# Turning the adapter probabilities by a crossbar transpose in float16 pieces instead of on TensorE

## What is computed

```
xn  = layernorm(x)
q,k,v: 16 query heads of 16 channels share one key and one value head
att = softmax(q k^T) v, turned back to 256 channels, times Wo, plus bo
# adapter, six experts e with 100 rows l of rank 16: A (6,100,16), B (6,16,256)
tokens = A B                             # (e, l, c)
p      = softmax(xn tokens^T / 16)       # over the 100 rows, per expert
delta  = ((p[1:] val[1:]) + xn) wd^T + wd_b, times scale   # val = tokens wt^T + wt_b
ffn    = xn + log(exp(delta of the expert that the gate picks)), 0 replaced by eps
out    = x + att + ffn
```

## Time and profile before

| | |
|---|---|
| runs | 920.78, 924.08, 924.17 us |
| profiled execution | 922.81 us |
| its span (first to last instruction) | 921.0 us |
| mean granted TensorE clock | 0.971 of 2.4 GHz |
| busy: PE / DVE / ACT / POOL | 857.4 / 780.7 / 673.2 / 512.8 us |
| period of one batch, windows 1 to 13 | 52.40 us, 0.82 us a slot |

### The profile page before, as it was taken

How to read it: one execution, slowest core, us unless ns; L and a number is a source line. 1 busy time by engine, 2 the same in 40 slices (tenths; PEclk the granted TensorE clock), 3 DMA queues, 4 the chain that set the end, 5 groups by cost and what they waited for, 6 DMA issues and landing times.

```text
span 921.0 us, 17722 instructions
## 1 busy us (share of the span) xinstructions
PE 857.4 (93%) x5845; PEld 282.1 (31%) x5845; DVE 780.7 (85%) x1490; ACT 673.2 (73%) x1369; POOL 512.8 (56%) x691
## 2 busy tenths in 40 slices
PE   4479999999999999999999999999999999999895
PEld 2223222332323333332323333332333333232222
DVE  6578898988989898998989898998989898899814
ACT  2115787787878778777877877787778778788880
POOL 2656566565666656565666647566666656534200
PEclk9676999999999999999999999999999999999998
DMA  3423243534524453543335353442444453331110
GB/s 96 97 66 60 74 92 92 117 83 116 113 75 105 107 114 94 124 87 108 95 94 111 94 116 87 129 100 86 96 113 104 104 115 84 92 94 61 48 60 34
DMA packets 125072, 86.04 MB, mean 93 GB/s; under 512 B 57143, under 2 KB 109112, under 8 KB 124984
## 3 DMA queue, kind: packets, MB, share of 16 engines
q1 hardware_dynamic: 124824, 84.82, 38.3%
q10 hardware_dynamic: 160, 0.10, 0.1%
HBM read 39.30 MB, written 33.54 MB: 79 GB/s over the span
## 4 chain that ended last, share of the span: by engine, by line
PE 78%; DVE 15%; issue 3%; POOL 2%; ACT 1%; DMA 1%; ACTq 0%; POOLq 0%; DVEq 0%
PE pO L364 24%; PE pA L346 18%; DVE M L808 9%; PE pB L351 8%; PE pA L481 5%; PE pA L428 5%; PE pA L499 4%; PE pA L483 3%; PE pA L417 3%; PE pA L453 2%; PE pA L468 2%; DVE st L728 2%; PE pB L461 1%; DVE RL L821 1%; PE pB L439 1%
## 5 line engine op out<-in xcount | busy, mean ns | idle before, releaser
L808 DVE TENSOR_REDUCE M<-pA 128x1 f32<-128x512 f32 x1024 | 652.3, 682 | 86.4 <-PE pA L346 82.3
L627 ACT ACTIVATE P<-pB 128x512 f32<-128x512 f32 x1002 | 552.6, 601 | 130.5 <-PE pB L351 126.0
L346 PE MATMUL pA<-K,Q 48*128 48x512 f16 x1024 | 326.0, 388 | 21.7 <-DVE M L808 11.8
L351 PE MATMUL pB<-Q,K 50*128 50x512 f16 x1002 | 317.8, 385 | 0.3 <-DVE M L808 0.3
L364 PE MATMUL pO<-P,VK 128*32 128x512 f32 x2048 | 273.7, 607 | 3.1 <-ACT OTr L633 2.0
L346 PEld LDWEIGHTS pA<-K,Q 48*128 48x128 f16 x1024 | 67.8, 94 | 343.6 <-DVE M L808 287.7
L954 POOL TENSOR_SCALAR Cz<-Cx 128x512 f32<-128x512 f32 x32 | 62.1, 1940 | 37.0 <-ACT Cx L609 37.0
L499 PE MATMUL pA<-wo,On 128*128 128x256 f32 x248 | 71.9, 414 | 2.7 <-DVE RL L821 2.7
L364 PEld LDWEIGHTS pO<-P,VK 128*32 128x32 f32 x2048 | 40.4, 108 | 99.3 <-issue 63.2
L351 PEld LDWEIGHTS pB<-Q,K 50*128 50x128 f16 x1002 | 64.3, 94 | 11.8 <-ACT P L627 10.3
L968 POOL TENSOR_TENSOR On<-Op,Rb 128x512 f32<-128x512 f32 x31 | 39.9, 1286 | 45.0 <-issue 41.2
(11 more groups left out here) (148 smaller groups left out, 806.6 us busy)
## 6 DMA issues: line engine op xcount, KB each, us to landing
o_parts<-OTr SPq DMA_DIRECT2D x62, 256.0 KB, 2.3
X<-in_x SPq DMA_DIRECT2D x16, 512.0 KB, 3.9
q_pieces<-Qp SPq DMA_DIRECT2D x64, 128.0 KB
out<-OUT SPq DMA_DIRECT2D x32, 256.0 KB, 3.9
Op<-o_parts SPq DMA_DIRECT2D x31, 256.0 KB
Rb<-l_parts SPq DMA_DIRECT2D x31, 256.0 KB
Q<-q_pieces SPq DMA_DIRECT2D x30, 256.0 KB, 4.8
Q<-q_pieces SPq DMA_DIRECT2D x34, 128.0 KB, 4.5
```

What stands on the lines that cost most here:

```text
L346: e.matmul(bank1("ab", t)[:, :], Q16[r:r + 48, b % 3, h, 128 * s:128 * s + 128], K16[r:r + 48, b % 3, :], start=True, stop=True).then_inc( ...
L351: e.matmul(bankB(t)[:, :], K16[r:r + 50, b % 3, 128 * i:128 * i + 128], Q16[r:r + 50, b % 3, :, 32 * hh:32 * hh + 32], start=True, stop=Tr ...
L627: e.activation(P[:, u % PR, :], bankB(u + LB)[:, :], ACT.Exp, scale=alpha).then_inc(S("e"))
L808: e.tensor_reduce(M[:, t // 32 % 2, t % 2, t % 32 // 2:t % 32 // 2 + 1], bank1("ab", t)[:, :], AX, ALU.max, negate=True).then_inc(S("mx"))
```

## The change

En is split in two float16 pieces by two more GpSimd instructions inside `snorm` (a cast and a subtraction) into EP, 128 x 2 x 4 x 128; a new step `pd` on SP, slot 52.2 (12.6 for the first batch), turns EP by one crossbar transpose of 8 blocks to PT; `a` becomes three float16 products of 512 columns with the pieces of A. The steps `p` (TensorE) and `pte` (ScalarE) are gone, and with `p` one turn of the pB ring per batch. A power-of-two scale for the pieces is worked in: VectorE's sums are multiplied by 2^-11 before the reciprocal, VectorE's mask product takes one more factor, the largest element of A joins the search for the scale at the start, and GpSimd splits A once, in the step `ams` at slot -30, behind `utm` of batch 0. The load of Am_s moves from SP to ScalarE's queue.

```diff
-    "smax": -20.4, "sexp": -18.8, "ssum": -17.4, "snorm": -16.2, "p": -13, "pte": -12.4, "a": -5, "mm": -4.4,
+    "smax": -20.4, "sexp": -18.8, "ssum": -17.4, "snorm": -16.2, "pd": -11.8, "a": -5, "mm": -4.4,
...
# TensorE
-                if (b := due("p", n)) is not None:
-                    w.wait_ge(*before2("p", b))
-                    w.wait_ge(S("en"), b + 1)
-                    for i in range(4):
-                        mm = e.transpose(bank2("p", b)[0:NL, 128 * i:128 * i + 128], En[:, i, :], idf[:, :])
-                    mm.then_inc(S("pt"))
                 if (b := due("a", n)) is not None:
                     w.wait_ge(*before1("a", b))
-                    w.wait_ge(S("pte"), b + 1)
-                    w.wait_ge(S("am"), 16)
-                    e.matmul(bank1("a", b)[0:ER + 1, :], Am_s[0:NL, :], PT[0:NL, :],
-                             start=True, stop=True).then_inc(S("ma"))
+                    w.wait_ge(S("ptd"), 16 * (b + 1))
+                    w.wait_ge(S("amp"), 2)
+                    for k, (ap, pp) in enumerate(PIECES):
+                        mm = e.matmul(bank1("a", b)[0:ER + 1, :], AmP[0:NL, ap, :], PT[0:NL, pp, :, :],
+                                      start=(k == 0), stop=(k == 2))
+                    mm.then_inc(S("ma"))
...
# ScalarE
+            w.wait_ge(S("am0"), 1)
+            e.dma_start(Am_s[1:NL, 0:ER], Am[1:NL, :]).then_inc(S("am"), 16)
...
-                if (b := due("pte", n)) is not None:
-                    w.wait_ge(S("pt"), b + 1)
-                    w.wait_ge(S("ma"), b)
-                    e.copy(PT[0:NL, :], bank2("p", b)[0:NL, :]).then_inc(S("pte"))
...
# VectorE
+                    e.memset(amx[:, 1:2], 0.0).then_inc(S("am3"))
+                    w.wait_ge(S("am"), 16)
+                    w.wait_ge(S("am3"), 1)
+                    e.tensor_reduce(amx[0:NL, 1:2], Am_s[0:NL, 0:ER], AX, ALU.max,
+                                    apply_absolute_value=True).then_inc(S("wm"))
...
                     w.wait_ge(S("en"), b)
+                    e.tensor_scalar(sL[:, :], sL[:, :], 2.0 ** -11, None, ALU.mult).then_inc(S("sl2"))
+                    w.wait_ge(S("sl2"), b + 1)
                     e.reciprocal(sR[:, :], sL[:, :]).then_inc(S("sr"))
...
-                    e.tensor_tensor(MmT[0:ER + 1, :], bank1("a", b)[0:ER + 1, :], mkT[0:ER + 1, :],
-                                    ALU.mult).then_inc(S("mm"))
+                    e.scalar_tensor_tensor(out=MmT[0:ER + 1, :], in0=bank1("a", b)[0:ER + 1, :], scalar=asc[0:ER + 1, 0:1],
+                                           in1=mkT[0:ER + 1, :], op0=ALU.mult, op1=ALU.mult).then_inc(S("mm"))
...
# GpSimd
                     w.wait_ge(S("sr"), b + 1)
-                    w.wait_ge(S("pt"), b)
                     e.tensor_tensor(En[:, :, :], Es[:, :, :], bc(sR[:, :], NL), ALU.mult).then_inc(S("en"))
+                    w.wait_ge(S("en"), b + 1)
+                    w.wait_ge(S("ptd"), 16 * b)
+                    w.wait_ge(S("ep0"), 1)
+                    e.tensor_copy(EP[:, 0, :, 0:NL], En[:, :, :]).then_inc(S("eh"))
+                    w.wait_ge(S("eh"), b + 1)
+                    e.tensor_tensor(EP[:, 1, :, 0:NL], En[:, :, :], EP[:, 0, :, 0:NL], ALU.subtract).then_inc(S("el"))
+
+                if due("ams", n) is not None:
+                    w.wait_ge(S("scl"), 1)
+                    w.wait_ge(S("am"), 16)
+                    w.wait_ge(S("amd"), 1)
+                    e.memset(asc[:, :], 2.0 ** -11).then_inc(S("asc"))
+                    w.wait_ge(S("asc"), 1)
+                    e.tensor_copy(asc[0:ER, :], scl[0:ER, 7:8]).then_inc(S("asc"))
+                    e.tensor_scalar(Am_s[0:NL, 0:ER], Am_s[0:NL, 0:ER], scl[0:NL, 3:4], None, ALU.mult).then_inc(S("asc"))
+                    w.wait_ge(S("asc"), 3)
+                    e.tensor_copy(AmP[0:NL, 0, :], Am_s[0:NL, :]).then_inc(S("amp"))
+                    w.wait_ge(S("amp"), 1)
+                    e.tensor_tensor(AmP[0:NL, 1, :], Am_s[0:NL, :], AmP[0:NL, 0, :], ALU.subtract).then_inc(S("amp"))
...
# SyncE
+                if (b := due("pd", n)) is not None:
+                    w.wait_ge(S("el"), b + 1)
+                    w.wait_ge(S("ma"), b)
+                    e.dma_start_transpose(PT[:, :, :, :].rearrange("p k i t -> p (k i) t"),
+                                          EP[:, :, :, :].rearrange("p k i n -> p (k i n)")).then_inc(S("ptd"), 16)
```

More of the change, by code:

```diff
@@ L53 @@
     "qs1": -50, "vg": -50, "vge": -49, "vt": -48, "vte": -47, "gate": -46, "mask": -45, "qw1": -40, "mkd": -39,
-    "utm": -30, "s": 5, "smax": 5.6, "sexp": 6.2, "ssum": 6.8, "snorm": 7.4, "p": 13, "pte": 13.6, "a": 17, "mm": 17.6,
+    "utm": -30, "s": 5, "smax": 5.6, "sexp": 6.2, "ssum": 6.8, "snorm": 7.4, "pd": 12.6, "a": 17, "mm": 17.6,
     "d0": 21, "dexp0": 21.6, "d1": 25, "dexp1": 25.6, "guard0": 26.8, "dlog0": 30.2, "radd0": 31.6,
@@ L70 @@
     "rngq": -92, "rng": -88, "rg": -87, "xt0": -86.9, "xt1": -86.8, "xh0": -86.7, "xh1": -86.6, "two": -86.5, "xl0": -86.2,
-    "bs": -86, "scl": -85.8, "xl1": -85.6, "wh": -85.4, "wl": -85.2, "alpha": -60, "qra": -53.5, "qrb": -38, "wdh": -35, "scd": -35,
+    "bs": -86, "scl": -85.8, "xl1": -85.6, "wh": -85.4, "wl": -85.2, "alpha": -60, "ams": -30, "qra": -53.5, "qrb": -38, "wdh": -35, "scd": -35,
     "bw0": -34, "bwe0": -33.4, "bw1": -33.8, "bwe1": -33.3, "w2": -25, "w2e": -24.4, "w2s": -24.2,
@@ L79 @@
 PARTH_LAST = {"lr": 86.2, "or": 86.3, "rec": 88.8, "lw": 89.4, "rb": 92.2, "on": 98.3}
-PE_NAMES = ("ab", "pv", "rg", "xt0", "xt1", "bs", "bw0", "bw1", "w2", "uk", "q0", "q1", "vg", "vt", "s", "p", "a", "d0", "d1",
+PE_NAMES = ("ab", "pv", "rg", "xt0", "xt1", "bs", "bw0", "bw1", "w2", "uk", "q0", "q1", "vg", "vt", "s", "a", "d0", "d1",
             "d2", "d3", "mt", "o0", "o1", "o2", "o3", "sl0", "sl1", "oa0", "oa1", "oa2", "oa3", "ob0", "ob1", "ob2", "ob3")
-ACT_NAMES = ("root", "xh0", "xh1", "wh", "wdh", "kd", "alpha", "bwe0", "bwe1", "w2e", "qe0", "qe1", "vge", "vte", "sexp", "pte", "dexp0",
+ACT_NAMES = ("root", "xh0", "xh1", "wh", "wdh", "kd", "alpha", "bwe0", "bwe1", "w2e", "qe0", "qe1", "vge", "vte", "sexp", "dexp0",
              "dexp1", "dexp2", "dexp3", "dlog0", "dlog1", "mte", "ex", "ot")
@@ L88 @@
 POOL_NAMES = ("var", "refine", "norm", "ph", "pl", "w2s", "residual", "ks", "qs0", "qs1", "mask", "utm", "snorm", "guard0", "guard1", "radd0",
-              "radd1", "ms", "on")
-SP_NAMES = ("load", "xtd", "mkd", "kd", "qw0", "qw1", "qra", "qrb", "qread", "md", "ow", "lr", "or", "lw", "rb", "st0", "st1")
+              "radd1", "ms", "on", "ams")
+SP_NAMES = ("load", "xtd", "mkd", "pd", "kd", "qw0", "qw1", "qra", "qrb", "qread", "md", "ow", "lr", "or", "lw", "rb", "st0", "st1")
 def slots():
@@ L200, in build @@
         En = sb("En", [128, 4, NL])
-        PT = sb("PT", [128, T])
+        EP = sb("EP", [128, 2, 4, 128], F16)
+        PT = sb("PT", [128, 2, 4, 128], F16)
+        AmP = sb("AmP", [128, 2, ER + 1], F16)
+        asc = sb("asc", [128, 1])
         MmT = sb("MmT", [128, T])
@@ L243, in build @@
         wmx = sb("wmx", [128, 3])
-        amx = sb("amx", [128, 1])
+        amx = sb("amx", [128, 2])
         bmx = sb("bmx", [128, 3])
@@ L285, in build @@
             "ab": lambda t: (S("e"), t - LB + 1), "vg": lambda b: (S("vge"), b + 1),
-            "vt": lambda b: (S("gt"), b + 1), "p": lambda b: (S("pte"), b + 1),
+            "vt": lambda b: (S("gt"), b + 1),
             "mt": lambda g: (S("mte"), g + 1), "bw0": lambda b: (S("bwe"), 1), "bw1": lambda b: (S("bwe"), 2),
@@ L389, in _ @@
                     w.wait_ge(S("two"), 1)
-                    e.matmul(bank1("bs", 0)[:, 0:7], one[:, :], fac[:, 0:7], start=True, stop=True).then_inc(S("bs"))
+                    e.matmul(bank1("bs", 0)[:, 0:8], one[:, :], fac[:, 0:8], start=True, stop=True).then_inc(S("bs"))
                 for h in range(2):
@@ L667, in _ @@
                                     apply_absolute_value=True).then_inc(S("wm"))
-                    w.wait_ge(S("wm"), 6)
-                    e.tensor_tensor(wmx[:, 2:3], amx[:, :], wmx[:, 0:1], ALU.max).then_inc(S("wm"))
+                    e.memset(amx[:, 1:2], 0.0).then_inc(S("am3"))
[3 more added lines that the diff above has]
+                                    apply_absolute_value=True).then_inc(S("wm"))
                     w.wait_ge(S("wm"), 7)
+                    e.scalar_tensor_tensor(out=wmx[:, 2:3], in0=amx[:, 0:1], scalar=amx[:, 1:2], in1=wmx[:, 0:1],
+                                           op0=ALU.max, op1=ALU.max).then_inc(S("wm"))
+                    w.wait_ge(S("wm"), 8)
                     e.scalar_tensor_tensor(out=rng[:, :], in0=wmx[:, :], scalar=float(C), in1=bmx[:, :],
@@ L691, in _ @@
                     e.tensor_scalar(fac[:, 4:5], two[:, 2:3], 2.0 ** -22 / XS, None, ALU.mult).then_inc(S("t0"))
-                    w.wait_ge(S("t0"), 7)
+                    e.tensor_scalar(fac[:, 7:8], two[:, 2:3], 2.0 ** -33, None, ALU.mult).then_inc(S("t0"))
```

(8 more changed lines are left out.)

## The result

The changed kernel takes 976.11 us (median of 4 runs, 973.18 to 978.48) against 923.74 us: a ratio of 1.0573, 95% interval 1.0536 to 1.0609. Its profiled execution has a span of 976.7 us, 55.7 us more than before; the mean granted clock fell from 0.971 to 0.933. The forecast was slower, by 21.6 us, to 945, with a range of 932 to 960: the sign was right and the amount was far off.

The account below looks back on a forecast made before the run. The prediction took the bound as TensorE's chain, held at slot 59 by GpSimd's Cx through ScalarE's logarithm and exponential. 13 windows x 1.54 = +20.0, window 0 +0.8, window 14 -0.4, start +1.2: +21.6, said as 945 us, range 932 to 960.

Parts of the forecast that it names:

- GpSimd: Cast and subtraction ahead of XP, Cz, Cx: 1.63 us a window; with VectorE's 0.21, Cx ends 1.84 later.
- Granted clock: Closing wrong-if sign: the clock might fall in TensorE's new gaps and add time; no size or chance given.
- `a` shrinks by 0.30: Product with A on TensorE, behind slot 59's wait: 0.73 us against 1.03, 0.30 gained a window (0.2 to 0.4).
- TensorE gains at most 0.93 ahead of the stand: Transposes gone before A of slot 59: at most 0.93 us a window, but TensorE then waits there for ScalarE.
- the rival of 906 us: TensorE's gain shows in full because the hand-over from Cx to slot 59 does not bind: 906 us; rival's chance 8%.
- its half, 915: Half of TensorE's full gain shows: 915 us, within the same 8% rival.
- The turn: Crossbar transpose issued on SP lands after 4.7 us, costing nothing; late-turn rival, beyond 6.8 us, 14%.
- Given back: Rival: VectorE or ScalarE catches up part of the delay, ending within 0.5% of before, say 926 us; 6%.
- the forecast's -0.4: Window 14, which has no XP: slack absorbs the lateness and the shorter product gains, -0.4 us in all.
- Start: Before the steady windows: `ams` about 1.4 us, scale search +0.35, first batch's savings -0.6; together +1.2 us.

Follow-up runs that it names:

- e4: Changed kernel plus eight float16 products per window on TensorE, results unused, ahead of the tile of slot 59: 950.91 us, ratio 1.0302.
- e3: Kernel before with only the cast and subtraction added on GpSimd, nothing reading their results: 960.23 us, ratio 1.0413.
- e1: Changed kernel with GpSimd's XP (low piece of the normed x) moved from slot 49 to 52, behind Cx: 926.04 us, ratio 1.0039.
- e12: Kernel before with XP later on GpSimd, the four transposes and ScalarE's copy deleted, the product reading a constant PT: 913.27 us, ratio 0.9902.
- e5: Changed kernel with ScalarE's logarithm moved from slot 56.2 to 59.2 and the residual addition from 57.6 to 60: 927.35 us, ratio 1.005.
- e10: Changed kernel with XP, logarithm and the start's split of A moved later, product with A left at slot 59: 921.87 us, ratio 1.0015.
- e11: Kernel before with XP on GpSimd and the logarithm on ScalarE moved later: 919.21 us, ratio 0.9973.

## Why the prediction was right or wrong

- **GpSimd.** Right to hundredths: cast 0.52 (0.54 said), subtraction 0.95 (0.93), VectorE 0.21 (0.21), Cx 1.81 late (1.84), A of slot 59 at Cx + 1.29. e4's windows give +1.56, e3's +1.6.
- **Granted clock: the step that failed.** The prediction said TensorE would stand 2.8 us a window and summed all its work at full clock; the fall stood only in the last sentence, as something that "would add", without a price or a chance. It fell in every one of 13 windows. e4 gives back 25 us by filling the stand; by windows, a short fall costs 55.7 - 53.96 = 1.7 us and a long one about 3. The kernel before did show what a stand can do: at its start six products of 512 columns take 2.72 us behind a wait of 7.15 us, and 1.40 later. Nearer to the case is its end, where TensorE stood four times for 1.35 to 2.71 us and the clock fell for 3.4 us within 0.6 us behind two of them (rows below the list). The row that I read, a window at 1.00, was one without a stand of that length. A case "clock falls behind the stand" at half of 3.4 us a window would have put 945 + 13 x 1.7 = 967 beside 945; at the 3.2 us of the long falls, seen only afterwards, it is 987.
- **`a` shrinks by 0.30.** Not seen in the changed kernel, since the fall begins there; at full clock, in e1, pair to pair is 0.75 against 1.03, so 0.28.
- **TensorE gains at most 0.93 ahead of the stand.** The sum gave it no value, but it made the stand 2.8 us long where 2.19 was measured (1.81 of lateness and some 0.4 gained), and the rival of 906 us rested on it. e12 shows 0.41; the rest goes into waits for ScalarE. With nothing at all in the turn's place and XP moved as well the kernel gets to 913; the shorter product would make it some 909, an estimate from e1's 0.28 in 15 windows. So 906 was out of reach; its half, 915, is not ruled out by this.
- **The turn.** 4.7 us as taken, next to no cost in the changed kernel (one wait, 0.3 us), and as said only because of the stand. Where the stand is gone it is the next thing late (e1, e5, e10): by up to some tenths in most windows, and by 1 to 3 us in those where the reading back ahead of it on SP's queue is held up. The prediction took SP as free in every window from the one row of window 8. The Trainium skill's 1309 ns for each 128 x 128 crossbar transpose ("VectorE: DVE Perf Modes", The three transpose paths) does not add up block by block here: eight land in 4.7 us. The Trainium skill's advice (same page, Rules for kernel authors), TensorE where PSUM will do as the destination, agrees with e10 against e11, which has XP and the logarithm moved too: 921.9 against 919.2.
- **Given back.** It was not: windows 1 to 13 of e3 and e4 carry the whole lateness round. The +2.6 at window 14 in the sum below is the forecast's -0.4 and some 3.0 for the long fall that begins behind window 13's stand.
- **Start.** `ams` cost 1.6 us (1.4 said). The scale's search took 0.5 more (0.35 said), but it was made good before UTm and cost nothing. The first product with A starts at 56.12, before at 54.25: +1.9 where +1.2 was said.

The sum with what was measured: at the first product +1.9, windows 0 and 1 +2.7, twelve windows of 56.4 on average +48, window 14 +2.6, the end +0.5: 55.7 us. Of the twelve's 4.0 each, 1.56 is lateness, as in e4, and 2.4 the clock. The forecast's own sum for the median is 944.4 + 1.3 = 945.7, where it says 945; that changes nothing.

TensorE behind a stand near the end of the kernel before, and the clock a microsecond later:

```profile
902.15 1.19 PE L499 MATMUL pA<-wo,On 128*128 128x256 f32 x2 [2.71 <-DVE RL L821]
```

```profile
903.00:904.00 1.00, 1.00 (x4) 0.73 (x4) 0.00 (x0) 0.00 (x0) 0.00 (x0) 0.50 0.28 97
```

## What to carry to other kernels

Find the engine whose lateness another waits for at the place of the change, however low its mean load: 1.5 us a batch on an engine that was 56% busy cost 38 us of 922 by itself (e3), and 52 with the rest of the change. Where a forecast puts a stand of a microsecond or two on TensorE into a loop, give the fall of the clock behind it a price of its own. Before giving up the change look at what stands in the queues between, since one step moved on GpSimd, or the logarithm on ScalarE, took some 50 us back; but move the same steps in the kernel before too, since that is the fair rival. A transfer that replaces work on an engine also inherits the waits of the queue it is put in.

## What was not expected of the hardware

A stand of 2.2 us at full clock was enough: the granted clock went to 1.2 GHz between 0.4 us before and 1.0 us after TensorE started again, and stayed there for 3.4 us, or twice that. In the changed kernel the two kinds differ in when the fall came: the six short ones began 0.7 to 1.0 us after the restart, the seven long ones between 0.4 us before it and 0.1 us after it. In e3, with stands of 1.6 us (2.1 once), the clock fell behind seven of thirteen; in e4, where the added work left 0.5 us of the stand (0.9 once), behind two. What decides when the fall comes, and so its length, stays open, as does whether the turn ahead of Lc on SP's queue would be in time without making VectorE wait for Lc; neither was tried.
